# First layer of a macaron megakernel: VectorE makes the bf16 terms of the row maxima, GpSimd's waits for landings stand at a batch's beginning, and the first batch's second-half products stand in the gate stage

## The reference

```python
x = x + 0.5 * _L0_ffn_ref(_layernorm(x), ...)     # dense product + top-2 of 8 low-rank experts
x = x + _L0_attn_ref(_layernorm(x), ...)          # 16 heads of width 16, LoRA projections
x = x + 0.5 * _L0_ffn_ref(_layernorm(x), ...)
x = x + 0.5 * _L1_ffn_ref(_layernorm(x), ...)     # 32 experts, top 4, given indices: rows are sorted by expert
x = x + _L1_attn_ref(_layernorm(x), ...)          # latent attention
x = x + 0.5 * _L1_ffn_ref(_layernorm(x), ...)
# _L0_attn_ref: scores = einsum('bhqd,bhkd->bhqk', q, k) * SCALE; attn = softmax(scores); out = attn @ v
```

## Time and profile before

| | |
|---|---|
| median of 3 runs | 1677.49 us (1675.85 to 1683.42) |
| profiled execution | 1681.14 us, span 1679.3 us |
| PE busy | 1254.7 us (75%) |
| DVE busy | 922.2 us (55%) |
| ACT busy | 636.1 us (38%) |
| POOL busy | 568.3 us (34%) |
| mean granted PE clock | 0.843 of full speed |

### The profile page before, as it was taken

How to read it: one execution, slowest core, us unless ns; L and a number is a source line. 1 busy time by engine, 2 the same in 40 slices (tenths; PEclk the granted TensorE clock), 3 DMA queues, 4 the chain that set the end, 5 groups by cost and what they waited for, 6 DMA issues and landing times. The chain is left out here.

```text
span 1679.3 us, 20929 instructions
## 1 busy us (share of the span) xinstructions
PE 1254.7 (75%) x5912; PEld 761.1 (45%) x5912; DVE 922.2 (55%) x2625; ACT 636.1 (38%) x1678; POOL 568.3 (34%) x621
## 2 busy tenths in 40 slices
PE   5669888748686179993289849966997699289990
PEld 3332333213233068882145625543555355278880
DVE  6777467437372212226579449935982696122327
ACT  2115444424343035552046305611660265045550
POOL 1063632642633325551022014302420332335550
PEclk8788989878787579997589959986997699689995
DMA  3755470730303174546000000000000000144447
GB/s 101 113 95 170 76 188 19 111 135 14 123 18 151 50 242 163 155 154 199 27 1 1 0 4 26 23 1 10 23 20 0 13 26 14 50 141 155 156 143 259
DMA packets 81473, 141.53 MB, mean 84 GB/s; under 512 B 15364, under 2 KB 63653, under 8 KB 78805
## 3 DMA queue, kind: packets, MB, share of 16 engines
q1 hardware_dynamic: 61845, 97.83, 21.3%
q0 software_dynamic: 17408, 42.00, 7.1%
q10 hardware_dynamic: 2112, 0.38, 0.1%
HBM read 76.92 MB, written 63.00 MB: 83 GB/s over the span
## 5 line engine op out<-in xcount | busy, mean ns | idle before, releaser
L138 POOL DMA_INDIRECT outs_dram<-m_ys,dest x192 | 184.0, 958 | 173.0 <-ACT m_ys L996 157.9
L753 DVE TENSOR_REDUCE a_mx<-a_psU 128x1 f32<-128x512 f32 x256 | 165.4, 684 | 138.5 <-PE a_psU L384 119.8
L1016 DVE TENSOR_TENSOR m_hm<-m_psG,m_sg 128x128 f32<-128x128 f32 x192 | 56.0, 292 | 296.8 <-ACT m_sg L990 168.4
L1278 ACT ACTIVATE a_pr<-a_psA,a_nb 128x512 f32<-128x512 f32 (+3 forms) x256 | 132.5, 524 | 205.6 <-DVE a_nb L1392 205.6
L1060 PE MATMUL m_psG<-arena,m_xgT 128*128 x768 | 207.2, 393 | 0.5 <-issue 0.2
L1212 PE MATMUL a_psA<-a_kT,a_q 128*128 128x512 f32 (+3 forms) x512 | 183.4, 470 | 8.1 <-ACT a_pr L1278 7.9
L536 ACT ACTIVATE a_P<-a_psS 128x512 f32<-128x512 f32 x256 | 143.6, 597 | 106.8 <-PE a_psS L395 84.1
L138 POOL DMA_INDIRECT rows_dram<-a_xd,slot x128 | 127.2, 994 | 136.4 <-DVE a_xd L124 56.8
L1326 POOL TENSOR_TENSOR a_q<-a_q,a_t 64x512 f32<-64x512 f32 x64 | 80.6, 1259 | 237.1 <-DVEq L1385 215.7
L1060 PEld LDWEIGHTS m_psG<-arena,m_xgT 128*128 128x128 f32 x768 | 134.2, 195 | 16.7 <-issue 3.9
L384 PE MATMUL a_psU<-arena 96*128 96x512 bf16 x256 | 108.1, 429 | 38.6 <-DVE a_mx L753 36.4
(11 more groups left out here) (229 smaller groups left out, 2103.0 us busy)
## 6 DMA issues: line engine op xcount, KB each, us to landing
m_xg<-rows_dram SPq DMA_DIRECT2D x48, 512.0 KB
arena<-part_dram SPq DMA_DIRECT2D x96, 128.0 KB
rows_dram<-arena SPq DMA_DIRECT2D x12, 1024.0 KB
arena<-in_mo_w SPq DMA_DIRECT2D x6, 2048.0 KB
m_xg<-outs_dram SPq DMA_DIRECT2D x16, 512.0 KB, 4.3
m_ys<-outs_dram SPq DMA_DIRECT2D x16, 512.0 KB, 4.8
part_dram<-a_part SPq DMA_DIRECT2D x16, 384.0 KB
outs_dram<-m_ys,dest POOLq DMA_INDIRECT x192
```

Of the source, the lines that this page charges most:

```text
L138: pool.indirect_dma_start(out=rows_dram, out_offset=bass.IndirectOffsetOnAxis(ap=slot[:, c:c + 1], axis=0), in_=row, in_offset=None).then_ ...
L753: dve.tensor_reduce(mx[g % 2][:, 4 * kt + qt:4 * kt + qt + 1], psU[n % 2][:, :], AX, ALU.max).then_inc(u_free, 1)
L1278: ins = act.activation(pr[s % 2][:, AT[t]:AT[t] + (t + 1) * P], psA[:, AT[t]:AT[t] + (t + 1) * P], ACT.Exp, bias=nb[s % 2][:, t:t + 1], sc ...
```

## The change

1. **Maxima.** `maxima(g)` leaves POOL. DVE makes the three terms (`split_maxima`) at p % 8 = 2, ahead of `normalise`, and ACT issues its three transfers at p % 8 = 4 instead of 3.
2. **POOL's list.** It starts at i = 0. Per i it is now: terms of batch i+1, `bias(i)`, `route` (whole, at i = 0), `rows(i - 2)` whole, `entries` (24, 20, 20 at i = 1, 2, 3). The waits for landings stand ahead of `terms` at i = 2 and ahead of `bias` at i = 3, and once at the very end.
3. **First batch.** At i = -1 the q/k products 2 and 3 move from places 5, 6 to 12, 13 and both v products to 13. Their terms on DVE move to 14 and 15. The prefix sum `scan` moves from place 14 to 2, the rest of the routing sums (`bases`) from i = -1, p = 19 to i = 0, p = 5.

```diff
-    MX, TO, NRM, MAXROWS = (0, 8, 16, 24), (1, 9, 17, 25), (2, 10, 18, 26), 3
+    MX, TO, NRM, SPLIT, MAXROWS = (0, 8, 16, 24), (1, 9, 17, 25), (2, 10, 18, 26), 2, 4
-    QSC, QLN, QT, QK, QV = 0, 1, 2, 3, 7
+    QSC, QLN, QT = 0, 1, 2
+    QK, QV = {b: (3, 4, 5, 6) if b else (3, 4, 12, 13) for b in range(B)}, {b: (7, 8) if b else (13, 13) for b in range(B)}
...
-                if i == -1 and p == QK + 2:
+                if i == -1 and p == 5:
                     absorb(4, 8)
...
+            def split_maxima(g):
+                dve.wait_ge(nm_ready, g + 1)
+                if g >= 1:
+                    dve.wait_ge(max_in, 48 * g)
+                split3(dve, link, nm[:, :], nrest[:, :], mpart[:, 0:P], mpart[:, P:2 * P], mpart[:, 2 * P:3 * P], mpart_ready)
...
+                if p % 8 == SPLIT and live(g - 1):
+                    split_maxima(g - 1)
                 if p in NRM and live(g - 3):
                     normalise(g - 3)
...
                 if i == -1 and p == QT:
                     absorb(0, 4)
                     first_rows(1)
-                if i == -1 and QK < p <= QK + 4:
-                    terms(p - QK - 1)
-                if i == -1 and p == QK + 2:
+                    scan()
+                if i == -1 and p in (4, 5, 14, 15):
+                    terms((4, 5, 14, 15).index(p))
+                if i == -1 and p == 6:
                     absorb(4, 8)
-                if i == -1 and p == F1 + 7:
-                    scan()
-                if i == -1 and p == F1 + 12:
+                if i == 0 and p == 5:
                     dve.tensor_scalar(weight[:, :], weight[:, :], 0.5, None, ALU.mult)
                     bases()
...
-            def maxima(g):
-                pool.wait_ge(nm_ready, g + 1)
-                if g >= 1:
-                    pool.wait_ge(max_in, 48 * g)
-                split3(pool, step, nm[:, :], nrest[:, :], mpart[:, 0:P], mpart[:, P:2 * P], mpart[:, 2 * P:3 * P], mpart_ready)
-                pool.wait_ge(mpart_ready, g + 1)
...
-            for i in range(-2, B + 2):
+            ENTRIES = (0, 0, 24, 44, 64)
+            for i in range(0, B + 2):
                 b = i + 1
-                if live(4 * i - 1):
-                    maxima(4 * i - 1)
-                if 1 <= b < B:
+                if b < B:
+                    if i >= 2:
+                        pool.wait_ge(entered, 16 * ENTRIES[i])
+                    if i >= 3:
+                        pool.wait_ge(placed[(i - 3) % 2], 16 * TPB * TOPK * ((i - 3) // 2 + 1))
                     for c in range(4):
                         terms(b, c)
-                for q, lo, hi in ((0, 0, 4), (1, 4, 10), (2, 10, 16)):
-                    if 0 <= i - 2 < B:
-                        rows(i - 2, lo, hi)
-                    if live(4 * i + q):
-                        maxima(4 * i + q)
-                    if i == 0:
-                        route(q)
-                    if i in (1, 2, 3):
-                        n = 22 + 21 * (i - 2)
-                        entry(n + 7 * q if i > 1 else (0, 8, 15)[q], n + 7 * q + 7 if i > 1 else (8, 15, 22)[q])
-                    if q == 0 and 0 <= i < B:
-                        bias(i)
+                if i < B:
+                    if i == B - 1:
+                        pool.wait_ge(entered, 16 * ENTRIES[i])
+                        pool.wait_ge(placed[(i - 3) % 2], 16 * TPB * TOPK * ((i - 3) // 2 + 1))
+                    bias(i)
+                if i == 0:
+                    route()
+                if 0 <= i - 2 < B:
+                    rows(i - 2)
+                if 1 <= i <= 3:
+                    entries(ENTRIES[i], ENTRIES[i + 1])
+            for b in (B - 2, B - 1):
+                pool.wait_ge(placed[b % 2], 16 * TPB * TOPK * (b // 2 + 1))
```

More of the change, by code:

```diff
@@ L204, in main_units @@
             out += [("l",) + ffn_at(i, p, 8) + (c,) for c in range(2)]
[L205 to L208, removed]
+        if 0 <= i + 1 < B:
+            out += [("qk", i + 1, c) for c in range(4) if QK[i + 1][c] == p]
+            out += [("v", i + 1, u) for u in range(2) if QV[i + 1][u] == p]
         if p == OP and 0 <= i - 1 < B:
@@ L762, in _, with route @@
             pool.memset(V[:, :].rearrange("p (n c) -> p n c", c=32)[:, :, HD:HD + 1], 1.0).then_inc(v_padded, 1)
[L764 to L788, removed]
+            def route():
+                pool.wait_ge(drained, CHUNKS)
+                pool.wait_ge(scanned, 1)
+                pool.wait_ge(based, 1)
+                step(pool.tensor_tensor(cums, cums, run, ALU.add))
+                step(pool.tensor_tensor(ec(cums), ec(cums), off.unsqueeze(2).to_broadcast([P, NE, NC]), ALU.add))
+                step(pool.tensor_tensor(cums, cums, hot, ALU.mult))
+                n = W
+                while n > NC:
+                    n //= 2
+                    step(pool.tensor_tensor(cums[:, 0:n], cums[:, 0:n], cums[:, n:2 * n], ALU.add))
+                pool.tensor_copy(slot[:, :], cums[:, 0:NC]).then_inc(slots_ready, 1)
+                pool.wait_ge(slots_ready, 1)
+                pool.memset(zero, 0.0).then_inc(zeroed, 1)
             def bias(b):
@@ L806, in terms, with rows @@
                 pool.wait_ge(part_ready, n + 1)
-            def maxima(g):
-                pool.wait_ge(nm_ready, g + 1)
-                if g >= 1:
-                    pool.wait_ge(max_in, 48 * g)
-                split3(pool, step, nm[:, :], nrest[:, :], mpart[:, 0:P], mpart[:, P:2 * P], mpart[:, 2 * P:3 * P], mpart_ready)
-                pool.wait_ge(mpart_ready, g + 1)
-            def rows(b, lo, hi):
-                if b == 0 and lo == 0:
+            def rows(b):
+                if b == 0:
                     pool.wait_ge(rows_clear, 16 * 12)
-                for n in range(lo, hi):
+                for n in range(TPB * TOPK):
                     j = n // TOPK
@@ L821, in rows, with entries @@
                     scatter(pool, b * TPB * TOPK + n, slot, rows_dram, xd[:, j * D:(j + 1) * D], placed[b % 2])
-                if b < B - 1 or hi == TPB * TOPK:
-                    pool.wait_ge(placed[b % 2], 16 * (b // 2 * TPB * TOPK + hi))
-            for i in range(-2, B + 2):
-                b = i + 1
-                if live(4 * i - 1):
-                    maxima(4 * i - 1)
-                if 1 <= b < B:
+            def entries(lo, hi):
+                if lo == 0:
+                    pool.wait_ge(table_clear, 16)
+                    pool.wait_ge(place_ready, 1)
+                for c in range(lo, hi):
+                    scatter(pool, c, place, table_dram, number[:, c:c + 1], entered)
+            ENTRIES = (0, 0, 24, 44, 64)
+            for i in range(0, B + 2):
+                b = i + 1
+                if b < B:
[3 more added lines that the diff above has]
+                        pool.wait_ge(placed[(i - 3) % 2], 16 * TPB * TOPK * ((i - 3) // 2 + 1))
                     for c in range(4):
                         terms(b, c)
-                for q, lo, hi in ((0, 0, 4), (1, 4, 10), (2, 10, 16)):
-                    if 0 <= i - 2 < B:
-                        rows(i - 2, lo, hi)
-                    if live(4 * i + q):
-                        maxima(4 * i + q)
-                    if i == 0:
-                        route(q)
-                    if i in (1, 2, 3):
-                        n = 22 + 21 * (i - 2)
-                        entry(n + 7 * q if i > 1 else (0, 8, 15)[q], n + 7 * q + 7 if i > 1 else (8, 15, 22)[q])
-                    if q == 0 and 0 <= i < B:
-                        bias(i)
+                if i < B:
[11 more added lines that the diff above has]
+                pool.wait_ge(placed[b % 2], 16 * TPB * TOPK * (b // 2 + 1))
         @block.sync
```

## The result

In the first comparison the changed kernel took 1746.81 us (median of four, 1741.55 to 1753.51) against 1676.67 us before: ratio 1.0413, 95% interval 1.0361 to 1.0465. It is slower by 4.1%; 1648 was forecast. The same kernel, unedited, took 1741.2 us in a later comparison (`h1_after`) and 1626.9 us in another (`f0_after`), beside a kernel before of 1675.2 and 1674.4 us. Both outcomes have to be explained.

The account below looks back on a forecast made before the run. POOL's landing waits were taken to stall all four engines through ACT's list. Terms -39.7 + 9 - 5 + 4 + 3 = -28.7 gave 1652.4 us, as a median 1648.8, said as 1648; range 1637 to 1660.

Parts of the forecast that it names:

- Landing waits, POOL's order, DMAs: POOL's transfers in the layer: the new order hides behind later batches' attention, tail unchanged, earlier clears cost 0.
- C: Rival, slower: POOL's indirect transfers hold off DVE's new split instructions, up to 0.96 us each; +14, median 1692 us; chance 0.05.
- POOL's waits: Place 19 of batches 1 to 3, place 11 of batch 2: PE's idle time from POOL goes, -39.7 us.
- First batch: Stretch ahead of the first maximum: it comes earlier as work moves away; gain of 5 us, bounds 3 and 6.5.
- Split on DVE, bases, routing: Added cost: DVE's terms of the maxima 9 us, bases beside POOL's terms 4, routing beside gates and first terms 3.
- rival B: DVE and POOL excluding each other costs more, in splits and first-batch terms; -13.7, median 1664 us; chance 0.12.
- Sum: Whole kernel: all terms together give -28.7 us against the profiled execution of 1681.1 us.
- A: Rival: scores at groups 11 and 15 wait for the maxima's landings; about -20, median 1657 us; chance 0.10.
- D: Rival: a_xT at place 19 waits for something other than POOL, gaps stay; 0 to -4, 1675 us; chance 0.05.

Follow-up runs that it names:

- h2: Changed kernel with landing waits put back after every 4 to 7 indirect transfers; 1662.2 us, ratio 0.9931 to the kernel before.
- g2: The kernel before, unedited, profiled again on a chip without late signals; its profiled execution took 1671.4 us.
- e4: The kernel before with only POOL's landing waits taken out of the portions, POOL still splitting the maxima; 1642.9 us, ratio 0.9783.
- m2: Changed kernel with a landing wait after every three transfers and the bases back before the first group; 1644.0 us, ratio 0.9804.
- m1: Changed kernel with a landing wait after every three indirect transfers, on a further chip; 1640.4 us, ratio 0.9795.
- k2: Changed kernel with a landing wait after every third transfer of either kind, on a chip with late signals; 1641.1 us, ratio 0.9758.
- k4: Changed kernel with three fills on POOL after every 4 to 7 transfers, no landing wait; 1656.3 us, ratio 0.9848.
- k3: Changed kernel with transfers handed out over three groups of a batch behind waits for their maxima, no landing wait; 1690.3 us, ratio 1.0072.
- k1: Changed kernel with landing waits after 4, 6 and 6 rows only, entries in runs of 24, 20 and 20; 1692.0 us, ratio 1.0070.

## Why the prediction was wrong, step by step

The step that failed is "Landing waits, POOL's order, DMAs", costed at 0 because "the rest hides behind the attention of later batches". I asked how busy POOL was, and not what a longer unbroken run of its transfers does to others. In the first comparison it cost about 113 us; on h1's chip, h2's runs of at most seven took 79 us back. It was not among the rivals either: C (POOL's transfers hold DVE's split off) has the right sign and the wrong mechanism. The split took 1.08 to 1.13 us in the midst of transfers as elsewhere. There was a sign: the trace of before holds waits of 2.4 and 3.6 us that ended "remote", at 205.87 and 430.35 us, right behind runs of eight and seven. The table of waits that I had read before predicting shows the second of them, and 4.1 us of the same kind for ACT; I passed over both.

The other steps, by a pair of traces without late signals on one chip (g2, span 1669.6; f0, 1628.0):

- **POOL's waits.** -39.7 forecast. Groups 5, 9, 10 and 14 are 3.0, 8.9, 24.5 and 17.1 us shorter: -53.5. Mechanism right; more, since place 19 of that before stood 23.0 and 16.1 us, and since the clock is 1.00 in groups 9 and 10 instead of falling behind a gap. e4 shows the landing waits to be most of it (37 us of the whole). The rest needs the split off POOL: groups 10 and 14 are 30.9 and 29.8 us in e4, 20.6 and 20.6 in f0.
- **First batch.** -5 forecast; first maximum 76.7 to 69.8, -6.9 (first comparison: 77.8 to 71.8, -5.9). The size is uncertain by 2 us or so, as traces with this same start gave 68.1 to 71.8.
- **Split on DVE, bases, routing.** 9 + 4 + 3 = 16 forecast; all other groups together are 17.4 us longer, so rival B (29) falls too. Each split took 1.08 us, not 0.9, and 5.3 in group 0, beside the routing. By m2, what bases cost beside POOL's terms they save ahead of the first maximum, so of this pair no loss or gain can be told. The Trainium skill (SBUF — State Buffer, section Who interferes with whom) has certain DVE instructions, those with two SBUF inputs or in a two-port mode, and GpSimd's hold each other off for whole instructions; m1's rows agree, with 1.07 us for an instruction (L633) that took 0.18 in m2, where no terms ran beside it.
- **Sum.** -28.7 forecast, -41.6 measured between the two spans: 1627 where nothing is late is below my range, 1747 far above it. Of the -41.6, -53.5 - 6.9 + 17.4 make -43.0, which leaves 1.4 us for all that I had costed at 0: where nothing is late, that step was right within 1.4 us.
- **Rivals A and D** fall: the wait at place 19 went, and in none of the traces after, h1 and f0 did a score wait over 0.3 us for the landing of a_mpart.
- **Misread, with nothing hanging on it.** Slices 9 and 11 of the page have PE at four and six tenths, not at a third of 75%. POOL's list in this layer has 128 transfers (64 rows, 64 entries), not 192. Rival C turns slower from 0.59 us a wait, not 0.65: -39.7 + 14 + 2 + 40 x 0.59 is 0.

**What stays open.** Why a long run makes PE's signals late, and why on some chips and not on others: two (and that of the first comparison, if it was a third) with, two without, and one on which only runs of three were tried. No run here shows a resource that both use. The Trainium skill (DMA: Bandwidth & Descriptors, section SWDGE vs HWDGE vs iDMA) says that GpSimd writes the descriptors of its transfers into rings in SBUF, which is where TensorE's operands lie too; none of the runs can show that they meet there. That it is tied to the chip, and not to what else ran beside it at the time, is also not separated.

## What to carry to other kernels

Don't let GpSimd issue indirect transfers in long unbroken runs beside work that is paced by TensorE's signals: break them after about three by a wait for their landing. At runs of seven, some 2 us of other work did as well as such a wait; at three it was not tried. Against the unbroken list where nothing is late this is 0.8% (1640 on one chip, 1627 on another; never side by side). A wait that looks like pure loss may be a throttle: before it goes, look at what the table of waits says of signals that come late with it there. And compare on more than one chip before a change is judged, since a steady interval within one comparison said nothing of the next here.

## What the hardware showed that was not expected

- While POOL issued indirect transfers in a long run, PE's signals kept DVE waiting up to 22.4 us (26.6 in h1), with a DMA share of 0.10 in one such stretch; the signals of DVE, ACT and POOL came within 0.01 us of the end of their instruction.
- It grows with the run: against the 23.4 us of group 5 without late signals, three in a row cost 0 us, seven or eight 3 to 5 us, twenty-four 22 to 25 us. The largest delay of a PE signal behind its product's recorded end was 0.25 us with runs of three (k2), 3.1 to 4.3 with seven or eight (k4, the kernel before, h2), 8.2 with 17 (k3), 17.7 with 24 (k1), and 27.4 and 28.1 with 36 (the changed kernel, h1).
- One kernel, unedited, differed by 7% between chips (1627 and 1747 us), while the kernel before stayed within 0.6% (1671 to 1680).
